# New order numbers for all stages of a two-layer gated attention and expert kernel

## The reference, cut to what matters

```python
x = x + tanh(g_xattn[0]) * L0_xattn(layernorm(x), ctx)   # q, k layernormed per head, softmax, v, Wp
x = x + tanh(g_ffn[0])   * tanh(layernorm(x) @ W @ A1 @ A2 + bias)
x = x + tanh(g_xattn[1]) * L1_xattn(layernorm(x), ctx)   # k, v = self rows and context rows, 8 heads x 64
x = x + tanh(g_ffn[1])   * L1_ffn(layernorm(x))          # top 2 of 8 experts, inner width 1024
...
probs = softmax(x @ gate_w.T); w, idx = top_k(probs, 2); w = w / sum(w)
acc = acc + ce[:, None] * (silu(g) * u @ dn.T)           # for each expert, ce its weight for the row
```

## Time and profile before

| | us |
|---|---|
| median of three runs | 598.37 (598.09 to 599.06) |
| the profiled execution, its own time | 598.98 |
| span of that execution in the trace | 597.2 |
| TensorE busy with matmuls | 569.6 (95%) |
| VectorE busy | 403.0 (67%) |
| ScalarE busy | 312.5 (52%) |
| GpSimd busy | 278.5 (47%) |
| mean granted TensorE clock | 0.993 |
| chain of work that ended last: TensorE, VectorE | 85%, 8% |

### The profile page before, as it was taken

The page is one execution under the profiler, slowest core; times in us unless marked ns, Lnnn a source line. Parts: engine busy times, 40 slices in busy tenths (PEclk is TensorE's granted clock), DMA queues, the critical chain, the costliest instruction groups (busy, mean ns, idle before and its releaser), DMA issues.

```text
span 597.2 us, 13760 instructions
## 1 busy us (share of the span) xinstructions
PE 569.6 (95%) x5606; PEld 485.7 (81%) x5606; DVE 403.0 (67%) x817; ACT 312.5 (52%) x602; POOL 278.5 (47%) x237
## 2 busy tenths in 40 slices
PE   8899999999989999999999999999899999999994
PEld 7676677777756887888888888977799999989994
DVE  7777568678777465768585765767676777746661
ACT  2445554564546455555464555556346567636641
POOL 3738558657721065547564656541301344421324
PEclk9989999999999999999999999999999999999998
DMA  8900660000000000000000000037182677636111
GB/s 265 353 25 2 262 237 3 2 2 2 2 2 2 1 1 2 9 1 24 2 24 2 25 24 1 23 125 315 34 253 85 215 245 256 190 93 228 29 20 25
DMA packets 24091, 50.93 MB, mean 85 GB/s; under 512 B 7072, under 2 KB 17104, under 8 KB 20688
## 3 DMA queue, kind: packets, MB, share of 16 engines
q1 hardware_dynamic: 18560, 45.20, 21.3%
q0 software_dynamic: 4224, 3.70, 3.4%
q10 hardware_dynamic: 1232, 1.01, 0.6%
HBM read 37.89 MB, written 13.31 MB: 86 GB/s over the span
## 4 chain that ended last, share of the span: by engine, by line
PE 85%; DVE 8%; ACT 2%; DMA 2%; issue 1%; POOL 1%; DVEq 0%; POOLq 0%; ACTq 0%
PE ps L59 15%; PE ps L60 14%; PE ps L61 14%; PE ps L745 5%; PE ps L603 5%; PE ps L715 5%; PE ps L727 5%; DVE KN L1114 4%; PE ps L585 4%; PE ps L675 3%; PE ps L665 2%; PE ps L619 2%; PE ps L564 2%; PE ps L522 1%; PE ps L539 1%
## 5 line engine op out<-in xcount | busy, mean ns | idle before, releaser
L1873 POOL TENSOR_SCALAR P<-P,rinv 112x487 f32<-112x487 f32 x56 | 88.4, 1589 | 60.4 <-DVE rinv L1147 60.4
L1816 POOL TENSOR_TENSOR sr<-sv,mhalf 125x32 f32<-125x32 f32 x13 | 71.1, 5470 | 1.1
L60 PE MATMUL ps<-XGf,WH 128*128 128x256 f32 x252 | 71.3, 283 | 0.0
L59 PE MATMUL ps<-XGf,WH 128*128 128x256 f32 x252 | 71.3, 283 | 0.0
L61 PE MATMUL ps<-XGf,WL 128*128 128x256 f32 x252 | 71.3, 283 | 0.0
L410 POOL DMA_INDIRECT out<-WS,rows_i x16 | 28.4, 1776 | 89.2 <-ACT WS L1719 85.9
L1114 DVE TENSOR_REDUCE KN<-ps 112x4 f32<-112x1500 f32 x32 | 55.0, 1719 | 19.4 <-PE ps L585 19.3
L1472 DVE TENSOR_TENSOR WL<-WR,WH 128x1024 fp32r<-128x1024 f32 x48 | 57.1, 1220 | 13.4 <-ACT WH L1773 9.8
L1635 ACT ACTIVATE P<-ps,nm 112x487 f32<-112x487 f32 x64 | 42.1, 663 | 42.6 <-DVE nm L1139 42.6
L1586 ACT ACTIVATE P<-ps 125x1344 f32<-125x1344 f32 x32 | 41.3, 1292 | 36.6 <-PE ps L603 36.5
L1139 DVE TENSOR_REDUCE nm<-ps 112x1 f32<-112x487 f32 x64 | 39.4, 656 | 21.4 <-PE ps L715 21.4
(11 more groups left out here) (271 smaller groups left out, 1520.4 us busy)
## 6 DMA issues: line engine op xcount, KB each, us to landing
WR<-in_gupT SPq DMA_DIRECT2D x16, 1024.0 KB, 7.2
WR<-in_dwnT SPq DMA_DIRECT2D x8, 1024.0 KB, 10.5
xs<-ZT SPq DMA_DIRECT2D x14, 516.0 KB, 6.0
CT<-in_ctxT SPq DMA_DIRECT2D x1, 2250.0 KB, 10.1
P<-xs SPq DMA_DIRECT2D x7, 256.0 KB, 10.8
P<-xs SPq DMA_DIRECT2D x9, 128.0 KB, 2.1
Wk<-in_L_xattn_Wk SPq DMA_DIRECT2D x2, 512.0 KB, 11.1
Wv<-in_L_xattn_Wv SPq DMA_DIRECT2D x2, 512.0 KB, 11.8
```

Source lines behind the costliest of these rows:

```text
L59: e.matmul(out, ah, bh, start=start, stop=False)
L60: e.matmul(out, ah, bl, start=False, stop=False)
L1816: e.tensor_tensor(sr[:, p, :], sv[:, p, :], mhalf[0:125, 0:32], ALU.pow).then_inc(s("sr"), 1)
L1873: e.tensor_scalar(P[:, k, 0:487], P[:, k, 0:487], rinv[:, k:k + 1], None, ALU.mult).then_inc(s("psc"), 1)
```

## The change

Every number in the tables is replaced. No instruction is added or removed, and no wait is edited; what changes is the place of stages in the list, and with it which stage gets which of the three shared banks. Of the diff the lines that the text speaks of:

```diff
-QUAD = ((-0.67, "S0"), (0.39, "max0"), (3.51, "qt2"), (3.49, "qt2c"), (8.05, "st"), (8.41, "ex"), (10.58, "V0"))
+QUAD = ((-0.61, "S0"), (-0.28, "max0"), (4.57, "qt2"), (4.69, "qt2c"), (8.21, "st"), (9.52, "ex"), (10.54, "V0"))
...
-VALUES = ((-14.97, "v", 1, 0), (-13.67, "vc", 1), (0.18, "v", 0, 0), (3.28, "v", 0, 1), (7.92, "vc", 0))
+VALUES = ((-15.32, "v", 1, 0), (-14.72, "vc", 1), (-1.56, "v", 0, 0), (4.25, "v", 0, 1), (5.33, "vc", 0))
...
-PAIR = ((-0.08, "S"), (3.03, "sc"), (8.97, "T"), (12.95, "V"))
+PAIR = ((0.04, "S"), (1.7, "sc"), (8.4, "T"), (13.08, "V"))
...
-TAIL_LAST = ((-4.88, "rv"), (1.55, "rb"), (7.42, "rbc"), (8.97, "aT"), (14.19, "wo"), (10.7, "res", 3),
-             (11.3, "stats", 3), (11.46, "norm", 3), (15.81, "xt", 3), (13.01, "xtc", 3), (19.61, "rt0"),
-             (18.84, "rt1"), (21.22, "rt2"), (24.77, "rt3"), (25.96, "rt4"), (29.91, "rt5"))
+TAIL_LAST = ((-1.61, "rv"), (1.0, "rb"), (1.77, "rbc"), (9.13, "aT"), (10.92, "wo"), (12.72, "res", 3),
+             (14.11, "stats", 3), (16.08, "norm", 3), (15.32, "xt", 3), (15.91, "xtc", 3), (31.03, "rt0"),
+             (30.17, "rt1"), (31.95, "rt2"), (40.43, "rt3"), (43.51, "rt4"), (60.85, "rt5"))
...
-SPLIT = ((13.47, "split", 0), (28.35, "low", 0), (13.78, "split", 1), (19.04, "split", 2), (34.62, "split", 3),
+SPLIT = ((8.86, "split", 0), (21.89, "low", 0), (19.33, "split", 1), (23.06, "split", 2), (87.31, "split", 3),
```

More of the change, by code:

```diff
@@ L109 @@
[L109 to L113, removed]
@@ L136 @@
-TAIL1 = ((10.22, "aT"), (15.01, "wo"), (13.29, "res", 3), (15.64, "stats", 3), (19.39, "norm", 3), (20.55, "xt", 3),
-         (20.53, "xtc", 3), (23.74, "rt0"), (24.13, "rt1"), (26.17, "rt2"), (27.81, "rt3"), (33.68, "rt4"),
-         (37.9, "rt5"))
-TAIL_NEXT = ((13.16, "aT"), (15.16, "wo"), (16.51, "res", 3), (20.39, "stats", 3), (22.9, "norm", 3),
-             (24.96, "xt", 3), (27.28, "xtc", 3), (28.79, "rt0"), (28.84, "rt1"), (28.94, "rt2"), (29.49, "rt3"),
-             (34.28, "rt4"), (39.89, "rt5"))
@@ L143 @@
-TAIL_LAST = ((-4.88, "rv"), (1.55, "rb"), (7.42, "rbc"), (8.97, "aT"), (14.19, "wo"), (10.7, "res", 3),
-             (11.3, "stats", 3), (11.46, "norm", 3), (15.81, "xt", 3), (13.01, "xtc", 3), (19.61, "rt0"),
-             (18.84, "rt1"), (21.22, "rt2"), (24.77, "rt3"), (25.96, "rt4"), (29.91, "rt5"))
+QUAD = ((-0.61, "S0"), (-0.28, "max0"), (4.57, "qt2"), (4.69, "qt2c"), (8.21, "st"), (9.52, "ex"), (10.54, "V0"))
+FIRST = ((-44.8, "stats0", 0), (-52.59, "rs0", 0), (-27.24, "wq", 0), (-26.92, "norm", 0, 0), (-26.22, "wq", 1),
[5 rows of a table added]
+         (-7.71, "spkc", 0, 0), (-6.05, "spk", 0, 1), (-5.97, "spkc", 0, 1), (-10.03, "stats0", 1),
+         (-8.23, "stats0", 2), (-11.3, "ksc", 0, 0), (-7.14, "qaff", 0), (-10.91, "spk", 0, 2),
+         (-7.41, "spkc", 0, 2), (-5.51, "spq", 0), (-3.13, "spqc", 0), (-17.21, "rs0", 1), (15.04, "rs0", 2),
+         (-15.04, "kp", 1, 1, 0), (-6.18, "kp", 1, 1, 1), (-5.58, "kq", 1, 1), (-0.39, "kss", 1, 1),
+         (-6.42, "norm", 1, 0), (-1.78, "xt", 1, 0), (-1.1, "xtc", 1, 0), (-0.41, "kp", 1, 0, 0),
+         (2.66, "kp", 1, 0, 1), (6.61, "kq", 1, 0), (6.25, "kss", 1, 0), (11.05, "ksc", 1, 1), (18.61, "spk", 1, 0),
+         (20.83, "spkc", 1, 0), (15.5, "spk", 1, 1), (17.48, "spkc", 1, 1), (7.34, "ksc", 1, 0), (13.2, "qaff", 1),
+         (13.04, "spk", 1, 2), (11.91, "spkc", 1, 2), (13.05, "spq", 1), (12.53, "spqc", 1))
@@ new lines @@
+PREP = ((-37.06, "cs"), (-44.3, "norm", 0), (-32.43, "kp", 1, 0), (-31.0, "xt", 0), (-32.7, "xtc", 0),
+        (-28.72, "kp", 1, 1), (-28.71, "kq", 1), (-25.9, "kss", 1), (-27.69, "kp", 0, 0), (-24.71, "kp", 0, 1),
+        (-20.36, "kq", 0), (-20.23, "kss", 0), (-23.18, "qg"), (-19.0, "ksc", 1), (-17.21, "spk", 0),
+        (-18.29, "spkc", 0), (-15.49, "spk", 1), (-13.24, "spkc", 1), (-11.35, "ksc", 0), (-12.11, "qaff"),
+        (-10.08, "spq"), (-11.06, "spqc"), (-6.71, "spk", 2), (-6.76, "spkc", 2))
@@ new lines @@
+VALUES = ((-15.32, "v", 1, 0), (-14.72, "vc", 1), (-1.56, "v", 0, 0), (4.25, "v", 0, 1), (5.33, "vc", 0))
+VALUES_1 = ((-12.59, "v", 1, 0), (-11.16, "vc", 1), (0.97, "v", 0, 0), (3.16, "v", 0, 1), (6.45, "vc", 0))
+TAIL0 = ((27.49, "ob"), (31.92, "obT"), (31.68, "aw"), (33.27, "awT"), (32.64, "aT"), (44.51, "wo"),
+         (45.56, "res", 1), (52.81, "stats", 1), (56.57, "norm", 1), (72.01, "xt", 1), (71.96, "xtc", 1),
+         (74.87, "f2"), (75.36, "res", 2), (76.74, "rtanh"), (77.46, "radd"), (77.83, "stats", 2), (80.9, "norm", 2),
+         (84.77, "xt", 2), (84.19, "xtc", 2))
@@ new lines @@
+TAIL1 = ((12.18, "aT"), (15.17, "wo"), (14.61, "res", 3), (15.98, "stats", 3), (20.4, "norm", 3), (21.95, "xt", 3),
+         (20.82, "xtc", 3), (23.4, "rt0"), (21.54, "rt1"), (26.29, "rt2"), (26.69, "rt3"), (35.35, "rt4"),
+         (36.91, "rt5"))
+TAIL_NEXT = ((12.89, "aT"), (17.63, "wo"), (15.59, "res", 3), (15.63, "stats", 3), (21.6, "norm", 3),
+             (22.28, "xt", 3), (26.93, "xtc", 3), (30.04, "rt0"), (28.95, "rt1"), (34.1, "rt2"), (38.88, "rt3"),
+             (41.54, "rt4"), (47.12, "rt5"))
```

33 lines of the change are left out of this document (8 added, 25 removed), and 19 rows, old and new, of tables (FIRST, FIRST1, PREP1).

## The result

The changed kernel takes **601.34 us** (median, 601.03 to 601.96), beside 598.40 us of the kernel before: ratio 1.0047 with a 95% interval of 1.0032 to 1.0062. It is 2.9 us slower, where I had forecast 596.7 and had put the end of the range at 600.3. Its profiled execution took 601.96 us, with a span of 600.1 against 597.2.

The account below looks back on a forecast made before the run. TensorE was taken as full in layer 1, so only waits elsewhere could close: -1.35 + 0.4 + 0 - 0.6, with 0.1 for spq(7), gave -1.65 and 596.7 us. The 8-in-10 range was 595.0 to 600.3.

Parts of the forecast that it names:

- Part 1, the start: Layer 0, batches 0 to 2: st(2) comes at 41.7 instead of 43.07, a gain of 1.35 us.
- S0(0) goes from 21.74 to about 21.0: Start of layer 0: TensorE's 0.79 us wait for norm(0,0) is filled, so the first scores start earlier.
- nothing, with 1 us of cover: Start, GpSimd: fill() and the first root chain come over 4 us later, but VectorE reaches their readers 1 us after that.
- The step on qaff(1): Start: GpSimd's line 1217 begins near 31.5, takes 2.74 us and ends near 34.25; st(1), behind spq(1), starts at 34.7.
- Part 2, layer 0: Layer 0's repeating batches: a loss of 1.35 us less gains of 0.8 and 0.15, so a cost of 0.4.
- the gain of 0.8 by wo and v: Layer 0: wo(b) moves between S0(4k) and st, v(b+2,0,0) takes its old place; 0.16 us gained five times.
- The 1.35 for res: Layer 0: res(b,1) behind max0(4k) delays VectorE's ksc and so S0(4k+1), a loss of 0.27 us five times.
- Part 3, layer 1: Layer 1: TensorE is full, so order cannot shorten it; zero change, V(12,0)'s copy in time with 0.19 us of cover.
- the rival that it misses: Layer 1: VectorE's copy comes too late for V(n,0) in batches 9 to 14; 599.8 or 603.1 us, chance 0.24.
- Part 4, the end: Way to the experts: gain 0.5 us from aT(14) ahead of T(15,1) and 0.1 from the router's place-finding.
- The router's term: Way to the experts: place-finding rt5(6) moves ahead of rt1(7); norm(7,3) to rt2(7) goes from 3.7 to 3.5, gain 0.1.
- the start gives nothing: Rival: the clock stays at 1.2 GHz for another stretch or qaff(1) grows later, start's gain 0; 598.1 us, chance 0.22.

Follow-up runs that it names:

- fill_back: The changed kernel with rs0(1) behind fill() on GpSimd again, the only queue that changes; 599.00 us, ratio 0.9994 to 1.0013 to the kernel before.
- spq_back: The changed kernel with TensorE's spq(1) and its copy behind V0(1) again; 598.85 us, ratio 0.9991 to 1.0011 to the kernel before.
- start_new: The kernel before with only the table of the start (FIRST) of the changed kernel; 602.26 us, ratio 1.0032 to 1.0065 to the kernel before.
- qg_back: The changed kernel with qg(b) behind kss(b,0) on GpSimd again; 600.83 us, ratio 1.0026 to 1.0048 to the kernel before.
- layer0_back: The changed kernel with qg(b) behind kss(b,0) again and res(b,1), wo(b), v(b+2,0,0) as before; 599.54 us, ratio 0.9997 to 1.0024.
- aT_first: The kernel before with one move, aT(14) ahead of T(15,1) on VectorE and ScalarE; 599.05 us, ratio 0.9986 to 1.0012.

## Why the prediction was wrong, point by point

**Part 1, the start (-1.35, measured +2.24).** st(2) was forecast at 41.7 and starts at 45.31, 3.6 us later. The step that failed is "S0(0) goes from 21.74 to about 21.0": it went to 22.57. I had seen that fill() would come over 4 us later, asked only who reads what it writes, and found "nothing, with 1 us of cover". I didn't ask what would run beside it. norm(1,0) was taken at 0.41 us and lasted 1.45, and fill_back shows the memset as the cause. The 0.8 us of the filled wait in front of it failed too, for another reason: the forecast counted a wait that had been taking up the scatter of the opening transposes, and in this trace they are 0.90 us longer. The step on qaff(1) was right in its duration (2.74 taken, 2.73 measured) and wrong in its start, 33.5 and not 31.5: behind the late S0(0) came the roots' step of 0.62. st(1) so came 2.2 us behind its forecast of 34.7. So spq(1) cost and did not gain, and spq_back puts that at 2.5 us. The last 1.4 us are the clock: 8.44 us from st(1) to st(2) and not 7.0. That is the bound I had given, one more stretch at the lower level on bound work for 1.5.

fill_back, whose opening transposes are as short as in the trace that I worked from, has S0(0) at 20.80, line 1217 at 31.43 and st(1) at 34.82, where the forecast had 21.0, 31.5 and 34.7. So the chain up to st(1) was worked out rightly but for what runs beside it. st(2) is at 43.26 even there, 1.6 behind the forecast, and the kernel at 599.0 has no gain at all.

The Trainium skill, page "SBUF — State Buffer", section "Who interferes with whom", says that VectorE in a two-port mode, which `tensor_scalar` can enter, and GpSimd shut each other out for the whole of an instruction, and that a VectorE instruction with two SBUF inputs contends with a GpSimd instruction that reads SBUF. The traces agree with both: a `tensor_scalar` beside a memset (0.41 to 1.45), and a multiply with two inputs beside qg (0.68 to 1.10), while a maximum out of PSUM stays at 1.72 us beside a memset. The Trainium skill, page "GPSIMD Engine Reference", section Specifications, names the two-port modes as well; the prediction took only the half on two inputs, and only to line 1217.

There it may have been set aside too soon. Line 1217's first one on GpSimd is 2.73 to 2.74 us in fifteen traces, but 1.96 in start_new, where VectorE's ksc(1,1) comes ahead of the maximum and not behind it:

```profile
32.75 1.96 POOL L1217 TENSOR_TENSOR KN<-KN,S 112x256 f32<-112x256 f32 x1 [1.73 <-DVE KN L1104]
```

In all sixteen it ends 0.59 us behind the end of ksc(1,1), a multiply with two inputs. So its length goes by where ksc(1,1) stands. What holds it before that multiply begins is open: the six later ones take 0.73 us beside the same maximum.

**Part 2, layer 0 (+0.4, measured +1.88).** The step that failed is the gain of 0.8 by wo and v, with the 0.15 by st(7). S0(4k) did come 0.15 us earlier each time, and st(7) another 0.15, but S0(4k+1) hangs on GpSimd's roots, which did not move with them, so nothing was kept. I had worked out that the time in front of S0(16) shrinks and not asked what S0(17) waits for. In qg_back, where res, wo and v stand as in after and qg as before, layer 0 is 1.24 us longer than before; against layer0_back, 1.47. The 1.35 for res is in that range, but no run moves res alone. And "qg before kss(b,0)" was in my list of things that cost nothing; it costs 1.94 us alone. The small term for spq(7), 0.1, isn't seen either: its wait went from 0.54 to 0.36 us, and S0(28) kept its distance to S0(27).

**Part 3, layer 1 (0, measured -1.25).** The chain to the copy was right, with more cover than worked out (0.47 us between its end and V(12,0), against 0.19), and the rival that it misses didn't come about. The step that failed is the sentence "Nothing that only changes the order can shorten this part", by which the term was put at nothing. Busy in every slice isn't the same as never waiting.

**Part 4, the end (-0.6, measured -0.51).** Right in sum and not shown in its parts. The term of 0.5 for aT(14) alone is worth nothing (aT_first); V(15,0) and V(15,1) have moved too in after, and no run tells whether aT(15) comes earlier by them. The router's term was right at 0.09 of 0.1. The end itself scatters by up to 0.9 us between executions of one order (32.66 to 33.57 with that of after). Where the clock doesn't fall in it, it is 32.66 to 33.12 with the order of after and 33.47 to 33.55 with that of before, so the gain stands. Where it falls, rt5(7) can wait for rt4(7) behind TensorE's warm-up transposes at a lower clock, as in spq_back:

```profile
426.30 0.17 DVE L1352 TENSOR_TENSOR r_u<-ps,base 112x8 f32<-112x8 f32 x1 [0.36 <-PE ps L822]
```

**The chances.** I gave the slower side 0.20, all of it to a miss in layer 1. The measured 601.34 lies between the 599.8 and the 603.1 of that rival, but by luck: no V(n,0) waits for its copy. The rival "the start gives nothing" was nearest in mechanism and too mild. It put the start at 0 at worst, and the start lost 2.2. Two sums of this part are slightly off: 596.7 and 3.0 make 599.7, and the shares as broken down make 0.18 for slower and 0.36 for same.

## What to carry to other kernels

When a step moves on one engine, list what will run beside it on the engine that it shares a port with, before and after, as carefully as the queues; one GpSimd instruction of 1.4 us beside a VectorE instruction of 0.4 took back 1.1 us here, more than the wait of 0.79 that the new order removed in front of it. A wait that disappears is a gain only if the next thing that waits was waiting for it: follow each gain to the next release by another engine, and look over several executions whether the wait was taking up a scatter. And test moves in the order that they came with: a swap that belongs to a gain lost 5 us when made alone, and two causes of which each is enough show nothing when one is undone.
